# The last stages of a graph and LSTM kernel: one comparison per half for the gates, H doubled on ScalarE and added on GpSimd, four output buffers

## The chip, the cores and the metric

The kernel runs on one core of one Trainium2 chip. The metric is the device time of one execution in microseconds; given are the median of three runs and, beside it, one profiled execution from which the trace comes.

## What is computed

The program takes 6250 nodes with 256 features, adds a graph aggregation with two dense layers and a linear attention, and puts an LSTM with a small head on top. The change concerns only the head behind the LSTM:

```python
lstm_out = _lstm(x, W_ih, W_hh, b_ih, b_hh)
logits = jnp.einsum('bth,lh->btl', lstm_out, W_lin) + b_lin        # two logits per node
g = argmax(logits, axis=-1)[..., None]                             # 0 or 1
w = g * lstm_out
inc = jnp.cumsum(w, axis=1)
prefix = inc - w
suffix = inc[:, -1:, :] - inc
return 2.0 * lstm_out + prefix * fw_att + suffix * bw_att
...
x = x + _L0_ffn_ref(_layernorm(x)[None], ...)[0]
```

In the code H is `lstm_out`, kept in `hs`; the `x` of the last line is kept, transposed, in `x1T`; the running sum `inc` is in `cum`.

## The kernel before

All of this is feature by node: 128 partitions hold half of the 256 features, and the second half (c = 1) lies behind the first in the free dimension. The 6250 nodes are cut in NB = 25 blocks of BN = 250. The LSTM is solved in CH = 125 chunks of LS = 50 steps side by side, so `hs` is stored by step: partition, step, half, chunk. Node n = 50 j + t stands at step t + 1, chunk j. Two steps of all chunks are 250 columns and make a block of the gates; a block of the results is 250 neighbouring nodes, that is 5 chunks with all their steps, read from `hs` with a step of 250 elements.

After the LSTM's sweeps, which run in a loop that ends on a flag, three stages follow. Each engine runs its own instruction stream in order, and semaphores counted by block join them.

The gates. L1588 writes the four weight tiles `lin_rep` (two logits, two halves), each weight repeated over 128 columns, so that a matmul gives a logit already spread over all partitions. TensorE (`logits`, L805 to L812) makes both logits of a block in one of two PSUM banks, four matmuls in fp32, each of which the trace shows as two passes. ScalarE (L1077) copies the first logit with its bias to `lg0`. VectorE compares (L1593) and multiplies each half of H by the result (L1596), writing into `cum` in the order of the nodes, with a step of 50 elements. VectorE waits for its own comparison ahead of the products and for its own products at the end of each block.

The running sums. L1605 is one scan over 6250 columns for each half, with a column of ones as the multiplier, and L1609 multiplies the totals by `bwc`.

The results. For each block ScalarE computes the suffix part, L1092, from `cum` with scale `nbw` and bias `tbw`, into one of two buffers. VectorE adds 2 H to x (L1616, one for each half), adds the prefix part (L1622, one for each half) and the suffix part (L1626, both halves). TensorE (`rows`, L821 to L829) transposes the sum back to nodes by features in four transposes into one of two PSUM banks, ScalarE copies the bank to one of two output buffers (L1100), and SyncE stores it (L391). `results` waits for TensorE two blocks back, `rows` for ScalarE two blocks back, `suffix` for VectorE two blocks back, and `rows_out` for the store two blocks back. On ScalarE the order is suffix(i+1), rows_out(i), suffix(i+2), and so on. GpSimd's last work is L473, long before.

Of the kernel before, what the change touches and what calls it, by code (L numbers as in the profile page):

```python
# [9 lines left out]
ALU = mybir.AluOpType  # L10
ACT = mybir.ActivationFunctionType
AX = mybir.AxisListType.X
ds = bass.ds

P = 128
# [42 lines left out]
def build(nc, a, out):  # L58
# [7 lines left out]
    with ExitStack() as ctx:  # L66
# [88 lines left out]
        lin_rep = wih[:, 0:4 * P].rearrange("p (a m) -> p a m", a=4)  # L155
# [46 lines left out]
        lg0, gsel = [scr[:, v * BN:(v + 1) * BN] for v in range(2)], scr[:, 512:512 + BN]  # L202
        suf, res = part[2:4], part[4:6]
        outs = [w[0:TP, :].rearrange("p (t d) -> p t d", d=D) for w in (wq, wk)]
# [15 lines left out]
        def bank(b, c=2, w=BN, parts=P):  # L220
# [17 lines left out]
            "pe_swept", "lin_v", "lg_mm", "lg_act", "lg_g", "lg_v", "cum_v", "suf_act", "t_v", "out_mm", "out_act", "out_st0", "out_st1")}  # L238
# [35 lines left out]
        def _(sp):  # L274
# [114 lines left out]
            def store(i, par):  # L389
                sp.wait_ge(S["out_act"], i + 1)  # L390
                sp.dma_start(out[ds(i * BN, BN), :].rearrange("(t p) d -> p t d", p=TP), outs[par]).then_inc(S[f"out_st{par}"], 16)  # L391
            with sp.Fori(0, (NB - 1) // 2) as r:
                for u in range(2):
                    store(2 * r + u, u)
            store(NB - 1, 0)
            sp.wait_ge(S["out_st0"], 16 * ((NB + 1) // 2))
            sp.wait_ge(S["out_st1"], 16 * (NB // 2))
# [3 lines left out]
        def _(pool):  # L401
# [70 lines left out]
            for c in range(2):  # L472
                pool.tensor_copy(whb[c], whhv[:, c, :]).then_inc(S["w_low"], 1)  # L473

        @block.tensor
        def _(pe):
# [172 lines left out]
            pe.wait_ge(S["eps1_v"], 2)  # L650
# [153 lines left out]
            pe.wait_ge(S["lin_v"], 1)  # L804
            def logits(i, par, first):  # L805
                if not first:
                    pe.wait_ge(S["lg_g"], i - 1)
                for l in range(2):
                    for k in range(2):
                        last = mm(psum[:, 6 + par, l * BN:(l + 1) * BN], lin_rep[:, 2 * l + k, :],  # L810
                                  hs[:, ds(2 * i + 1, 2), k, :], start=(k == 0), stop=(k == 1))
                last.then_inc(S["lg_mm"], 1)  # L812
# [8 lines left out]
            def rows(i, par, first):  # L821
                pe.wait_ge(S["t_v"], 4 * i + 4)
# [16 lines left out]
        def _(act):  # L839
# [233 lines left out]
            def logits(i, par, first):  # L1073
                act.wait_ge(S["lg_mm"], i + 1)
                if not first:
                    act.wait_ge(S["lg_g"], i - 1)
                fn(lg0[par], psum[:, 6 + par, 0:BN], ACT.Identity, bias=blc[:, 0:1]).then_inc(S["lg_act"], 1)  # L1077
            logits(0, 0, True)
            logits(1, 1, True)
            with act.Fori(1, (NB - 1) // 2) as r:  # L1080
                for u in range(2):
                    logits(2 * r + u, u, False)
            logits(NB - 1, 0, False)

            act.wait_ge(S["cum_v"], 5)

            def suffix(i, par):

                if not isinstance(i, int) or i >= 2:
                    act.wait_ge(S["t_v"], 4 * i - 4)  # L1090
# [5 lines left out]
            def rows_out(i, par):  # L1096
                act.wait_ge(S["out_mm"], i + 1)
                if not isinstance(i, int) or i >= 2:
                    act.wait_ge(S[f"out_st{par}"], 8 * (i - par))
                fn(outs[par], psum[0:TP, par, :].rearrange("p (t d) -> p t d", t=2), ACT.Copy).then_inc(S["out_act"], 1)  # L1100

            suffix(0, 0)
            for i in (1, 2):
                suffix(i, i % 2)
                rows_out(i - 1, (i - 1) % 2)
            with act.Fori(0, (NB - 3) // 2) as r:
                for u in range(2):
                    suffix(2 * r + u + 3, 1 - u)
                    rows_out(2 * r + u + 2, u)  # L1110
            rows_out(NB - 1, (NB - 1) % 2)

        @block.vector
        def _(dve):
# [487 lines left out]
            gate(NB - 1, 0, False)  # L1603
            for c in range(2):
                dve.tensor_tensor_scan(cum[:, c, 1:N + 1], ones[:, 0:1].broadcast_to([P, N]), cum[:, c, 1:N + 1], 0.0,  # L1605
                                       ALU.mult, ALU.add).then_inc(S["cum_v"], 1)
            dve.wait_ge(S["cum_v"], 3)
# [4 lines left out]
            def results(i, par, first):  # L1612
                if not first:
                    dve.wait_ge(S["out_mm"], i - 1)
                for c in range(2):
                    last = stt(res[par][:, c, :].rearrange("p (j t) -> p j t", t=LS),  # L1616
                               hs[:, 1:LS + 1, c, ds(i * (BN // LS), BN // LS)].rearrange("p t j -> p j t"), 2.0,
                               x1T[:, c, ds(i * BN, BN)].rearrange("p (j t) -> p j t", t=LS), ALU.mult, ALU.add)
                last.then_inc(S["t_v"], 1)
                dve.wait_ge(S["t_v"], 4 * i + 1)  # L1620
                for c in range(2):
                    stt(res[par][:, c, :], cum[:, c, ds(i * BN, BN)], fwc[:, c:c + 1], res[par][:, c, :],  # L1622
                        ALU.mult, ALU.add).then_inc(S["t_v"], 1)
                dve.wait_ge(S["t_v"], 4 * i + 3)
# [32 lines left out]
```

## Time and profile before

| | us |
|---|---|
| median of 3 runs (lowest, highest) | 2604.55 (2603.65, 2613.02) |
| profiled execution | 2609.78 |
| its span, first to last instruction | 2607.9 |
| VectorE busy, whole span | 1761.6 |
| TensorE busy, whole span | 2304.9 |
| ScalarE busy, whole span | 1521.7 |
| GpSimd busy, whole span | 118.7 |
| gates, 2449.2 to 2505.2 | 56.0 |
| running sums, 2505.2 to 2531.5 | 26.3 |
| results, 2531.5 to the end | 76.4 |

PE is TensorE, PEld its weight loads, DVE VectorE, ACT ScalarE, POOL GpSimd, SP SyncE; a trailing q means the engine's sequencer. Times in the rows below are microseconds from the span's start, durations of one instruction in nanoseconds where a mean is given. In a timeline a row is start, duration, engine, line, operation, output and input, count, and in brackets how long the engine had been idle and what released it. A matmul's end is modelled.

### The profile page before, as it was taken

The page shows a single profiled execution, that of the slowest core. Times are in us where ns is not written, and L with a number is a line of the kernel's source. Part 1 is how long each engine was busy: PE and PEld are TensorE (multiplying, and loading weights), DVE is VectorE, ACT ScalarE, POOL GpSimd, SP SyncE. Part 2 cuts the span into 40 slices and gives each one's busy share as a digit, 9 for nine tenths or more (in the row PEclk, how much of TensorE's full clock was granted, in tenths as well). Part 3 has the DMA queues.
Part 4 walks back from the last instruction along what each step waited for, and adds up shares of the span by engine and source line. Part 5 has one row for each costly group of instructions (what it writes and reads, how often), then busy time and mean ns, then how long its engine had stood idle before and what let it go on. Part 6 is the DMA issues. An engine that isn't in the chain of part 4 may idle for free.

```text
span 2607.9 us, 46559 instructions
## 1 busy us (share of the span) xinstructions
PE 2304.9 (88%) x14839; PEld 1974.3 (76%) x14839; DVE 1761.6 (68%) x4053; ACT 1521.7 (58%) x2861; POOL 118.7 (5%) x121
## 2 busy tenths in 40 slices
PE   4578989999999999999898999998887887888844
PEld 3467868888888888888786888888887887888623
DVE  5755887777777777777477455556665665566688
ACT  2354448888888888888533444445554555555315
POOL 4232000000000000000000000000000000000000
PEclk9889999999999999999999999999999999999975
DMA  3222320000000000000331122123332332333103
GB/s 96 70 70 79 97 74 25 27 26 24 27 25 28 23 28 26 29 23 21 108 95 44 63 86 86 79 89 116 110 115 82 110 117 87 106 114 110 39 8 90
DMA packets 95188, 174.13 MB, mean 67 GB/s; under 512 B 8983, under 2 KB 69411, under 8 KB 94769
## 3 DMA queue, kind: packets, MB, share of 16 engines
q1 hardware_dynamic: 63378, 86.63, 10.1%
q10 hardware_dynamic: 28108, 81.19, 9.9%
q0 software_dynamic: 3584, 4.76, 0.6%
q8 instruction: 72, 1.18, 0.2%
q14 instruction: 46, 0.38, 0.0%
HBM read 114.14 MB, written 58.36 MB: 66 GB/s over the span
## 4 chain that ended last, share of the span: by engine, by line
PE 62%; DVE 14%; issue 8%; ACT 5%; ACTq 2%; DVEq 1%; POOL 0%; DMA 0%; POOLq 0%
PE psum L608 22%; PE psum L603 11%; PE psum L758 9%; PE psum L718 8%; DVE scr L1535 3%; DVE scr L1533 2%; ACT scr L1018 2%; PE psum L726 2%; PE psum L660 2%; PE psum L670 2%; PE psum L714 2%; DVE scr L1357 2%; DVE scr L1531 1%; DVE bufB L1537 1%; ACTq L1029 1%
## 5 line engine op out<-in xcount | busy, mean ns | idle before, releaser
L931 ACT ACTIVATE counts<-psum 125x500 fp32r<-125x500 f32 (+1 forms) x663 | 720.1, 1121 | 160.9 <-PE psum L603 159.1
L608 PE MATMUL psum<-halves,counts 125*125 125x512 f32 x2500 | 743.9, 418 | 2.8 <-ACT counts L931 2.0
L1383 DVE TENSOR_TENSOR wx<-rs_buf 128x500 bf16<-128x500 bf16 (+2 forms) x1326 | 641.9, 531 | 132.0 <-PE psum L603 72.2
L758 PE MATMUL psum<-bufB,wx 128*128 x4800 | 603.9, 283 | 90.6 <-DVE bufB L1537 81.6
L758 PEld LDWEIGHTS psum<-bufB,wx 128*128 128x128 f32 x4800 | 565.3, 194 | 129.0 <-issue 118.1
L608 PEld LDWEIGHTS psum<-halves,counts 125*125 125x125 f32 x2500 | 418.6, 187 | 59.9 <-issue 4.8
L603 PE MATMUL psum<-wx 128*125 128x250 bf16 x2550 | 399.3, 277 | 5.5 <-DVE wx L1383 5.3
L603 PEld LDWEIGHTS psum<-wx 128*125 128x125 bf16 x2550 | 320.9, 139 | 91.0 <-DVE wx L1383 8.6
L718 PE MATMUL psum<-bufA,wx 128*128 (+1 forms) x1600 | 232.7, 289 | 0.0
L718 PEld LDWEIGHTS psum<-bufA,wx 128*128 128x128 f32 x1600 | 194.9, 192 | 23.6 <-issue 0.2
L1018 ACT ACTIVATE scr<-scr 128x125 f32<-128x125 f32 x300 | 92.2, 307 | 168.6 <-DVE scr L1535 168.6
L1537 DVE TENSOR_TENSOR bufB<-scr 128x125 f32 (+1 forms) x300 | 87.1, 290 | 146.6 <-ACT scr L1018 146.6
L1531 DVE TENSOR_TENSOR scr<-scr 128x125 f32<-128x125 f32 x300 | 85.8, 286 | 84.6 <-ACT scr L1011 84.4
L1006 ACT ACTIVATE psum<-bufA 128x500 f32<-128x500 f32 x144 | 85.7, 595 | 95.6 <-ACT scr L1018 95.5
L1011 ACT ACTIVATE scr<-psum 128x250 f32<-128x250 f32 x300 | 110.0, 367 | 31.6 <-PE psum L758 31.6
L1525 DVE COPY psum<-bufA 128x500 f32<-128x500 f32 x144 | 97.7, 678 | 30.2 <-issue 30.1
L1490 DVE COPY bufB<-psum 128x250 f32<-128x250 f32 x192 | 75.2, 415 | 61.1 <-PE psum L718 59.0
L1535 DVE TENSOR_TENSOR scr<-scr 128x125 f32<-128x125 f32 x300 | 87.1, 290 | 10.3
L827 PE MATMUL psum<-ident,scr 128*125 128x128 f32 x100 | 30.4, 459 | 70.4 <-DVE scr L1626 70.4
L987 ACT ACTIVATE scr<-psum 128x250 f32<-128x250 f32 x50 | 19.0, 379 | 125.2 <-PE psum L726 125.2
L1533 DVE TENSOR_TENSOR scr<-scr 128x125 f32<-128x125 f32 x300 | 86.1, 287 | 5.6 <-ACT scr L1013 1.4
L1013 ACT ACTIVATE scr<-psum 128x125 f32<-128x125 f32 x300 | 81.5, 272 | 6.7 <-PE psum L758 1.4
(257 smaller groups left out, 2464.8 us busy)
## 6 DMA issues: line engine op xcount, KB each, us to landing
bufA<-gates_of_x ACTq DMA_DIRECT2D x144, 500.0 KB, 3.4
gates_of_x<-bufB SPq DMA_DIRECT2D x48, 500.0 KB, 2.6
sums_by_feature<-scr SPq DMA_DIRECT2D x51, 125.0 KB, 2.0
x_times_eps_plus_sums<-rs_buf ACTq DMA_DIRECT2D x10, 625.0 KB
wx<-in_x_dram SPq DMA_DIRECT2D x25, 250.0 KB
x_plus_mix<-wx SPq DMA_DIRECT2D x25, 250.0 KB, 4.8
scr<-x_times_eps_plus_sums SPq DMA_DIRECT2D x50, 125.0 KB
x_times_eps_plus_sums<-scr SPq DMA_DIRECT2D x50, 125.0 KB
```

The lines of the kernel that those rows point to most:

```text
L603: last = mm(psum[0:TP, u % 3, g * KEYS:(g + 1) * KEYS], oh_l[r][:, g, :, t], oh_m[r][:, g, :, t], start=(t == 0), stop=(t == 1))
L608: return mm(psum[0:TP, 3 + v, :], cnt[v][:, hi, :], xhl[:, hi, :, :].rearrange("p s d -> p (s d)"), start=(hi == 0), stop=(hi == NT - 1))
L718: last = mm(gate_bank(u, m), wihv[:, c, m * P:(m + 1) * P], ls_in[:, ds(t, 1), c, :].rearrange("p t j -> p (t j)"), start=False, stop=Fals ...
L758: return mm(half_gates(u, m, slot[0])[:, slot[1], :], whhv[:, k, (2 * gate + m) * P:(2 * gate + m + 1) * P], h, start=False, stop=(k == 1) ...
L931: fn(cnt[v][:, :, 2 * GW * u:2 * GW * u + GW * g].rearrange("p h c -> p c h"), psum[0:TP, u % 3, 0:g * KEYS].rearrange("p (c h) -> p c h", ...
L1011: fn(half(s_if, m), half_gates(u, m, 1), ACT.Sigmoid).then_inc(S["hif_act"], 1)
L1018: fn(th[:, m * CH:(m + 1) * CH], tg_c[1 - u][:, 1, m * CH:(m + 1) * CH], ACT.Tanh).then_inc(S["hth_act"], 1)
L1383: last = tt(to[:, 0:gs, :, :], tab2[:, 0:k, :].unsqueeze(1).broadcast_to([P, gs, k, 2]), keysT[v][:, part_, g0:g0 + gs, :].unsqueeze(2).br ...
L1531: tt(prod[:, 1, cut], s_if[:, 1, cut], tg_c[u][:, 1, cut], ALU.mult)
L1533: tt(prod[:, 0, cut], s_if[:, 0, cut], tg_c[u][:, 0, cut], ALU.mult).then_inc(S["prod_v"], 1)
L1535: tt(tg_c[1 - u][:, 1, cut], prod[:, 0, cut], prod[:, 1, cut], ALU.add).then_inc(S["hc_v"], 1)
L1537: tt(hs[:, ds(t + 1, 1), m, :].rearrange("p t j -> p (t j)"), s_o[:, cut], th[:, cut], ALU.mult).then_inc(S["hh_v"], 1)
```

## The change

The two logits are not compared any more; their difference is. The weights become half the difference of the two rows of W_lin, `lin_rep` has two tiles in place of four, and the bias is compared with it, so that TensorE has two matmuls a block, and one VectorE operation for each half compares and multiplies. ScalarE no longer copies a logit. Instead it doubles `hs` in place, 25 operations of two steps each, ahead of the matmuls that read them, and `fwc` and `bwc` are halved early in the program since the sums are then doubled. GpSimd adds the doubled H to `x1T` in place, 50 operations of 250 columns, after the last doubling, and VectorE's L1616 goes. The ones of the scan are read from PSUM. ScalarE's and SyncE's loops are written out; output buffers are four in place of two, two of them in `wv` and `wp`.

```diff
-        lin_rep = wih[:, 0:4 * P].rearrange("p (a m) -> p a m", a=4)
+        lin_rep = wih[:, 0:2 * P].rearrange("p (a m) -> p a m", a=2)
+        lin_d, b_d = sb("lin_d", 2), sb("b_d", 1)
...
-        outs = [w[0:TP, :].rearrange("p (t d) -> p t d", d=D) for w in (wq, wk)]
+        outs = [w[0:TP, :].rearrange("p (t d) -> p t d", d=D) for w in (wq, wk, wv, wp)]
...
@@ gpsimd
+            pool.wait_ge(S["twice_act"], NB)
+            for i in range(NB):
+                cells = x1T[:, :, i * BN:(i + 1) * BN].rearrange("p c (j t) -> p c j t", t=LS)
+                for c in range(2):
+                    pool.tensor_tensor(cells[:, c, :, :], cells[:, c, :, :],
+                                       hs[:, 1:LS + 1, c, i * (BN // LS):(i + 1) * (BN // LS)].rearrange("p t j -> p j t"),
+                                       ALU.add).then_inc(S["xh_q"], 1)
@@ tensor
-            pe.wait_ge(S["lin_v"], 1)
+            pe.wait_ge(S["lin_v"], 3)
             def logits(i, par, first):
+                pe.wait_ge(S["twice_act"], i + 1)
                 if not first:
-                    pe.wait_ge(S["lg_g"], i - 1)
-                for l in range(2):
-                    for k in range(2):
-                        last = mm(psum[:, 6 + par, l * BN:(l + 1) * BN], lin_rep[:, 2 * l + k, :],
-                                  hs[:, ds(2 * i + 1, 2), k, :], start=(k == 0), stop=(k == 1))
+                    pe.wait_ge(S["lg_v"], i - 1)
+                for k in range(2):
+                    last = mm(psum[:, 6 + par, 0:BN], lin_rep[:, k, :], hs[:, ds(2 * i + 1, 2), k, :],
+                              start=(k == 0), stop=(k == 1))
                 last.then_inc(S["lg_mm"], 1)
@@ scalar
-                fn(lg0[par], psum[:, 6 + par, 0:BN], ACT.Identity, bias=blc[:, 0:1]).then_inc(S["lg_act"], 1)
...
-            act.wait_ge(S["cum_v"], 5)
+            for i in range(NB):
+                fn(hs[:, 2 * i + 1:2 * i + 3, :, :], hs[:, 2 * i + 1:2 * i + 3, :, :], ACT.Copy, scale=2.0).then_inc(S["twice_act"], 1)
+
+            act.wait_ge(S["cum_v"], 6)
...
+                if i >= 4:
+                    act.wait_ge(S[f"out_st{i % 4}"], 16 * (i // 4))
+                fn(outs[i % 4], psum[0:TP, i % 2, :].rearrange("p (t d) -> p t d", t=2), ACT.Copy).then_inc(S["out_act"], 1)
@@ vector
+                ts(cols[:, 8:12], cols[:, 8:12], 0.5, None, ALU.mult).then_inc(S["eps1_v"], 1)
+                dve.wait_ge(S["eps1_v"], 2)
                 ts(nbw[:, :], bwc, -1.0, None, ALU.mult).then_inc(S["eps1_v"], 1)
...
-            dve.tensor_copy(lin_rep, lin_c[:, :].unsqueeze(2).broadcast_to([P, 4, P])).then_inc(S["lin_v"], 1)
+            tt(lin_d[:, :], lin_c[:, 2:4], lin_c[:, 0:2], ALU.subtract).then_inc(S["lin_v"], 1)
+            tt(b_d[:, :], blc[:, 0:1], blc[:, 1:2], ALU.subtract).then_inc(S["lin_v"], 1)
+            dve.wait_ge(S["lin_v"], 2)
+            ts(lin_rep, lin_d[:, :].unsqueeze(2).broadcast_to([P, 2, P]), 0.5, None, ALU.mult).then_inc(S["lin_v"], 1)
             dve.memset(cum[:, :, 0:1], 0.0).then_inc(S["cum_v"], 1)
+            dve.memset(psum[:, 4, 0:1], 1.0).then_inc(S["cum_v"], 1)
 
             def gate(i, par, first):
-                dve.wait_ge(S["lg_act"], i + 1)
-                stt(gsel[:, :], psum[:, 6 + par, BN:2 * BN], blc[:, 1:2], lg0[par], ALU.add, ALU.is_gt).then_inc(S["lg_g"], 1)
-                dve.wait_ge(S["lg_g"], i + 1)
+
+                dve.wait_ge(S["lg_mm"], i + 1)
                 for c in range(2):
-                    last = tt(cum[:, c, 1:N + 1].rearrange("p (j t) -> p t j", t=LS)[:, ds(2 * i, 2), :],
-                              hs[:, ds(2 * i + 1, 2), c, :], gsel[:, :].rearrange("p (t j) -> p t j", t=2), ALU.mult)
+                    last = stt(cum[:, c, 1:N + 1].rearrange("p (j t) -> p t j", t=LS)[:, ds(2 * i, 2), :],
+                               psum[:, 6 + par, 0:BN].rearrange("p (t j) -> p t j", t=2), b_d[:, 0:1],
+                               hs[:, ds(2 * i + 1, 2), c, :], ALU.is_gt, ALU.mult)
                 last.then_inc(S["lg_v"], 1)
-                dve.wait_ge(S["lg_v"], i + 1)
...
-                dve.tensor_tensor_scan(cum[:, c, 1:N + 1], ones[:, 0:1].broadcast_to([P, N]), cum[:, c, 1:N + 1], 0.0,
+                dve.tensor_tensor_scan(cum[:, c, 1:N + 1], psum[:, 4, 0:1].broadcast_to([P, N]), cum[:, c, 1:N + 1], 0.0,
...
             def results(i, par, first):
                 if not first:
                     dve.wait_ge(S["out_mm"], i - 1)
+                dve.wait_ge(S["xh_q"], 2 * i + 2)
                 for c in range(2):
-                    last = stt(res[par][:, c, :].rearrange("p (j t) -> p j t", t=LS),
-                               hs[:, 1:LS + 1, c, ds(i * (BN // LS), BN // LS)].rearrange("p t j -> p j t"), 2.0,
-                               x1T[:, c, ds(i * BN, BN)].rearrange("p (j t) -> p j t", t=LS), ALU.mult, ALU.add)
-                last.then_inc(S["t_v"], 1)
-                dve.wait_ge(S["t_v"], 4 * i + 1)
-                for c in range(2):
-                    stt(res[par][:, c, :], cum[:, c, ds(i * BN, BN)], fwc[:, c:c + 1], res[par][:, c, :],
+                    stt(res[par][:, c, :], cum[:, c, ds(i * BN, BN)], fwc[:, c:c + 1], x1T[:, c, ds(i * BN, BN)],
                         ALU.mult, ALU.add).then_inc(S["t_v"], 1)
```

## Rows read from the trace of the kernel before

**Rows 1.** Windows: us, busy of each engine (instructions), granted clock, DMA share, GB/s

```profile
2449.20:2505.20 56.00, 50.20 (x200) 37.58 (x200) 39.33 (x75) 11.72 (x25) 0.00 (x0) 0.96 0.00 0
2505.20:2531.50 26.30, 0.00 (x0) 0.00 (x0) 26.25 (x3) 0.00 (x0) 0.00 (x0) 0.50 0.00 0
2531.50:2607.90 76.40, 30.38 (x100) 23.00 (x100) 64.25 (x127) 39.19 (x75) 0.00 (x0) 0.50 0.28 84
```

**Rows 2.** Waits, 2452 to 2608: engine line waited for, total us, times, longest

```profile
PE psum L827 <- DVE scr L1626: 70.4, 25, 32.4
```

**Rows 3.** Timeline of the gates, two blocks in the steady state

```profile
2480.65 0.48 DVE L1593 SCALAR_TENSOR_TENSOR scr<-psum,cols,scr 128x250 f32<-128x250 f32 x1
...
2481.38 1.10 DVE L1596 TENSOR_TENSOR bufA<-bufB,scr 128x250 f32 x2 [0.25 <-DVE scr L1593]
...
2482.89 0.48 DVE L1593 SCALAR_TENSOR_TENSOR scr<-psum,cols,scr 128x250 f32<-128x250 f32 x1 [0.41 <-DVE bufA L1596]
...
2483.53 3.91 PE L810 MATMUL psum<-bufB,wx 128*128 x16 [0.28 <-DVE scr L1593]
...
2484.84 0.48 DVE L1593 SCALAR_TENSOR_TENSOR scr<-psum,cols,scr 128x250 f32<-128x250 f32 x1
```

**Rows 4.** Timeline of the results, one block in the steady state

```profile
2539.79 1.08 DVE L1616 SCALAR_TENSOR_TENSOR scr<-bufB,bufC 128x250 f32 x2
...
2541.00 0.87 DVE L1622 SCALAR_TENSOR_TENSOR scr<-bufA,cols,scr 128x250 f32<-128x250 f32 x2
2541.34 0.60 ACT L1100 ACTIVATE wq<-psum 125x512 f32<-125x512 f32 x1 [1.40 <-PE psum L827]
2541.84 1.07 ACT L1092 ACTIVATE scr<-bufA,tbw,nbw 128x250 f32 x2
2541.99 0.68 DVE L1626 TENSOR_TENSOR scr<-scr 128x500 f32<-128x500 f32 x1
...
2542.62 1.08 DVE L1616 SCALAR_TENSOR_TENSOR scr<-bufB,bufC 128x250 f32 x2
...
2542.72 1.22 PE L827 MATMUL psum<-ident,scr 128*125 128x128 f32 x4 [1.51 <-DVE scr L1626]
```

**Rows 5.** Groups by line and shape, whole span: count, busy us, mean ns

```profile
L970 ACT ACTIVATE wq<-scr 128x500 f32<-128x500 f32 x13 | 8.1, 620 | 45.9 <-DVE scr L1448 45.9
...
L1605 DVE TENSOR_TENSOR_SCAN bufA<-ones,bufA 128x6250 f32<-128x6250 f32 x2 | 26.2, 13166 | 0.0
...
L1243 DVE TENSOR_TENSOR bufC<-bufB,tab 101x4000 bf16<-101x4000 f32 x2 | 9.0, 4521 | 0.0
...
L440 POOL TENSOR_TENSOR scr<-scr 125x256 f32<-125x256 f32 x50 | 37.4, 748 | 62.7 <-DVE scr L1296 60.8
```

**Rows 6.** Windows of the gates' first and later part, columns as in rows 1

```profile
2449.20:2453.00 3.80, 3.79 (x9) 3.16 (x10) 0.00 (x0) 0.05 (x1) 0.00 (x0) 0.50 0.00 0
...
2456.00:2480.00 24.00, 22.57 (x95) 16.72 (x94) 17.91 (x36) 5.62 (x12) 0.00 (x0) 1.00 0.00 0
```

**Rows 7.** Timeline of the gates' start, TensorE and ScalarE

```profile
2449.21 13.15 PE L810 MATMUL psum<-bufB,wx 128*128 128x250 f32 x48 [0.52 <-DVE wx L1588]
2452.95 0.47 ACT L1077 ACTIVATE scr<-psum,cols 128x250 f32<-128x250 f32 x1 [9.66 <-PE psum L810]
```

**Rows 8.** Timeline of an early stage where GpSimd and VectorE work together

```profile
96.78 0.73 POOL L440 TENSOR_TENSOR scr<-scr 125x256 f32<-125x256 f32 x1 [1.53 <-DVE scr L1296]
96.95 1.23 DVE L1241 TENSOR_TENSOR bufB<-bufB,tab 101x640 bf16<-101x640 f32 x1
```

**Rows 9.** Timeline of the results' first and last steps

```profile
2531.52 0.34 DVE L1609 TENSOR_SCALAR tbw<-bufA,cols 128x1 f32<-128x1 f32 x2
...
2533.78 0.68 DVE L1626 TENSOR_TENSOR scr<-scr 128x500 f32<-128x500 f32 x1
...
2600.93 0.68 DVE L1626 TENSOR_TENSOR scr<-scr 128x500 f32<-128x500 f32 x1
...
2603.54 0.27 SPq L391 DMA_DIRECT2D out_dram<-wq  x1
```

More of the change, by code:

```diff
@@ L200, in build @@
         dif = rs_buf[:, 1616 + G4:1616 + G4 + 4 * (CH - 1)].rearrange("p (a j) -> p a j", a=4)
-        lg0, gsel = [scr[:, v * BN:(v + 1) * BN] for v in range(2)], scr[:, 512:512 + BN]
         suf, res = part[2:4], part[4:6]
-        outs = [w[0:TP, :].rearrange("p (t d) -> p t d", d=D) for w in (wq, wk)]
+        outs = [w[0:TP, :].rearrange("p (t d) -> p t d", d=D) for w in (wq, wk, wv, wp)]
         psum = ctx.enter_context(nc.psum_tensor("psum", [P, 8, 512], F32))
@@ L237, in build @@
             "hif_mm", "hgo_mm", "hif_act", "htg_act", "hc_v", "hth_act", "hh_v", "fill_a", "fill_d",
-            "pe_swept", "lin_v", "lg_mm", "lg_act", "lg_g", "lg_v", "cum_v", "suf_act", "t_v", "out_mm", "out_act", "out_st0", "out_st1")}
+            "pe_swept", "lin_v", "lg_mm", "lg_v", "xh_q", "twice_act", "cum_v", "suf_act", "t_v", "out_mm", "out_act", "out_st0", "out_st1", "out_st2", "out_st3")}
         ld_x = [sem(f"ld_x{v}") for v in range(XR)]
@@ L387, in _ @@
                                  pre_out[v].rearrange("p g n -> p (g n)")).then_inc(S[f"pre_st{v}"], 16)
-            def store(i, par):
+            for i in range(NB):
                 sp.wait_ge(S["out_act"], i + 1)
[L391 to L397, printed above, removed]
+                sp.dma_start(out[i * BN:(i + 1) * BN, :].rearrange("(t p) d -> p t d", p=TP), outs[i % 4]).then_inc(S[f"out_st{i % 4}"], 16)
+            for v in range(4):
+                sp.wait_ge(S[f"out_st{v}"], 16 * ((NB + 3 - v) // 4))
         @block.gpsimd
@@ L649, in _ @@
             pe.wait_ge(S["ld_w12"], 32)
-            pe.wait_ge(S["eps1_v"], 2)
+            pe.wait_ge(S["eps1_v"], 3)
             def tail(i, par, inner=False):
@@ L821, in rows @@
             def rows(i, par, first):
-                pe.wait_ge(S["t_v"], 4 * i + 4)
+                pe.wait_ge(S["t_v"], 3 * i + 3)
                 if not first:
@@ L1071, in _ @@
                 act.reg_mov(go, act.value_load(flag[0:1, 0:1], min_val=0, max_val=CH))
[L1073 to L1076, printed above, removed]
-                fn(lg0[par], psum[:, 6 + par, 0:BN], ACT.Identity, bias=blc[:, 0:1]).then_inc(S["lg_act"], 1)
[L1078 to L1083, printed above, removed]
-            act.wait_ge(S["cum_v"], 5)
+            for i in range(NB):
+                fn(hs[:, 2 * i + 1:2 * i + 3, :, :], hs[:, 2 * i + 1:2 * i + 3, :, :], ACT.Copy, scale=2.0).then_inc(S["twice_act"], 1)
+            act.wait_ge(S["cum_v"], 6)
             def suffix(i, par):
                 if not isinstance(i, int) or i >= 2:
-                    act.wait_ge(S["t_v"], 4 * i - 4)
+                    act.wait_ge(S["t_v"], 3 * i - 3)
                 for c in range(2):
@@ L1094, in suffix, with rows_out @@
                 last.then_inc(S["suf_act"], 1)
-            def rows_out(i, par):
+            def rows_out(i):
                 act.wait_ge(S["out_mm"], i + 1)
[L1098 to L1111, printed above, removed]
+                if i >= 4:
+                    act.wait_ge(S[f"out_st{i % 4}"], 16 * (i // 4))
+                fn(outs[i % 4], psum[0:TP, i % 2, :].rearrange("p (t d) -> p t d", t=2), ACT.Copy).then_inc(S["out_act"], 1)
+            for i in range(NB + 1):
+                if i < NB:
+                    suffix(i, i % 2)
+                if i:
+                    rows_out(i - 1)
         @block.vector
@@ L1603, in _ @@
             gate(NB - 1, 0, False)
+            dve.wait_ge(S["lg_v"], NB)
             for c in range(2):
-                dve.tensor_tensor_scan(cum[:, c, 1:N + 1], ones[:, 0:1].broadcast_to([P, N]), cum[:, c, 1:N + 1], 0.0,
+                dve.tensor_tensor_scan(cum[:, c, 1:N + 1], psum[:, 4, 0:1].broadcast_to([P, N]), cum[:, c, 1:N + 1], 0.0,
                                        ALU.mult, ALU.add).then_inc(S["cum_v"], 1)
-            dve.wait_ge(S["cum_v"], 3)
+            dve.wait_ge(S["cum_v"], 4)
             for c in range(2):
@@ L1614, in results @@
                     dve.wait_ge(S["out_mm"], i - 1)
+                dve.wait_ge(S["xh_q"], 2 * i + 2)
                 for c in range(2):
[L1616 to L1622 removed]
+                    stt(res[par][:, c, :], cum[:, c, ds(i * BN, BN)], fwc[:, c:c + 1], x1T[:, c, ds(i * BN, BN)],
                         ALU.mult, ALU.add).then_inc(S["t_v"], 1)
[L1624 removed]
+                dve.wait_ge(S["t_v"], 3 * i + 2)
                 dve.wait_ge(S["suf_act"], i + 1)
```

## The prediction, made before the changed kernel was run

> **What bounds the kernel now.** Only the last 160 us of the program are touched, so I read those and nothing else. The busy times by stage come first [rows 1]: three stages stand there, the gates (56.0 us), the running sums (26.3 us) and the results (76.4 us). In the first, TensorE is busy 50.20 of 56.00 us, which looks like a TensorE bound; in the second only VectorE works; in the third VectorE is busy 64.25 of 76.40 us and everybody else waits, TensorE 70.4 us for L1626 [rows 2]. GpSimd does nothing in any of them.
>
> The timeline of the gates in their steady state [rows 3] corrects the first reading. Two blocks take 2484.84 - 2480.65 = 4.19 us, 2.10 a block. TensorE's 16 records for two blocks take 3.91 us, so 1.95 a block, and VectorE's own sequence is 0.48 (L1593), 0.25 idle, 1.10 (two L1596) and a turn of 0.12 (0.41 at the loop's end), so 1.95 to 2.24. VectorE is the one without slack, and TensorE would be there a moment later. Both have to shrink, and the change shrinks both.
>
> In the results [rows 4] a block takes VectorE 2542.62 - 2539.79 = 2.83 us: L1616 until L1622 starts 1.21, L1622 twice and a wait 0.99, L1626 until the next block 0.63. ScalarE has 0.50 (L1100) and 1.07 (L1092), TensorE 1.22 at half clock (0.50 in the stage's row [rows 1]).
>
> **Part 1, the preparation.** One copy (L1588) becomes two tiny subtractions, a wait and a scaling, with a one-element memset more. No such row stands in the last stages; from the gap of 0.25 between dependent VectorE operations [rows 3] I take 0.4 us more (bounds 0.1 and 0.8). The early halving of two vectors lies beside loads of the first microseconds: nothing, and at most 0.4 if that cover is gone.
>
> **Part 2, doubling on ScalarE.** 25 operations of 128x500 from SBUF to SBUF. The nearest row is L970, 620 ns [rows 5]. Since an operation starts 0.10 before the former's end (L1100 lasts 0.60, its follower starts after 0.50 [rows 4]), the pitch is 0.52, in all 13.0 us from about 2448.9 to 2461.9. ScalarE's 11.7 us of L1077 go in exchange. TensorE waits for the first doubling only, and that is over when the weights are written; later blocks are ready at 0.52 each while the stage needs over 1.0 each. No cost; if ScalarE started 1 us late, 1 us.
>
> **Part 3, the gates.** TensorE has two matmuls in place of four, so 0.98 a block at full clock. VectorE loses L1593 and has two operations with a PSUM input and the strided output of L1596. The trace has no such form. Lower bound for the pair: two plain ones, 0.87 (L1622 [rows 4]); upper: L1596 plus what the strided read adds in L1616, 1.10 + (1.08 - 0.87) = 1.31. I take L1596's 1.10, the same output pattern at the same length, because L1593 shows that a PSUM input costs nothing (0.48 against half of 0.87 plus an overlap). There are two PSUM banks, so block i+2 waits for the gate of block i; the loop is 0.98 (TensorE) + 0.25 (wait and register work ahead of VectorE) + 1.10 + 0.28 (VectorE to TensorE [rows 3]) = 2.61 for two blocks, 1.31 a block. VectorE alone would need 1.1, TensorE 0.98. With a little of the loop's turn I take 1.32 (bounds 1.05 and 1.60). The first two blocks run at 1.2 GHz: the first stretch has clock 0.50 and the later ones 1.00 [rows 6], and the first block's eight passes took from 2449.21 to 2452.95 [rows 7], so four take 1.87. Stage: 0.4 + 2 x 1.87 + 0.25 + 1.10 + 23 x 1.32 + 0.25 before the sums = 36.1 us, against 56.0: 19.9 saved.
>
> TensorE's clock: its busy share falls from 0.90 to about 0.98/1.32 = 0.74. At 1.2 GHz it would itself be the bound, busy without a gap, and it was from just such a stretch that it rose to 1.00 [rows 6].
>
> **Part 4, the sums.** The constant operand moves from SBUF to PSUM. L1605 takes 13166 ns for 6250 elements [rows 5], 2.11 ns each, where a tensor_tensor with two SBUF inputs runs at 4521/4000 = 1.13 (L1243), so it isn't the second input that slows it. Nothing gained or lost (bounds -1 and +1 us).
>
> **Part 5, GpSimd's 50 additions.** They start when all doublings are done, at 2461.9. L440, a tensor_tensor of 125x256, takes 0.72 us undisturbed (its mean of 748 ns has a few longer ones in it) [rows 5, 8]. The new one reads one input with a stride; on VectorE that turned a pair of 0.87 into 1.08 [rows 4], a factor of 1.25, so 0.90 (bounds 0.70 and 1.40, the second twice the plain one). 50 x 0.90 = 45 us: done at 2507. The results begin at 2449.2 + 36.1 + 26.3 + 0.3 = 2511.9. So the additions lie wholly beside gates and sums up to (2511.9 - 2461.9)/50 = 1.00 us apiece. Beyond that they don't merely deliver late (at 1.8 us a block and two operations a block they keep ahead up to 1.7), they collide with VectorE.
>
> That collision is in this trace: L1241, 640 columns with two SBUF inputs, took 1.23 us where L1243's rate gives 0.72; it had started 0.17 us into a GpSimd addition and ended 0.67 after it [rows 8]. It waited for GpSimd to end. The Trainium skill (SBUF — State Buffer, section "Who interferes with whom") says the same: a VectorE instruction with two SBUF inputs contends with a GpSimd one that reads SBUF, the pair of ports is a lock held for a whole instruction, and one with at most one SBUF input does not contend. The rule speaks against this change where GpSimd is still at it in the results, whose three operations all have two SBUF inputs, and for it in gates and sums, where one input now is in PSUM. No row here shows the second half. By the rule the sum stays what it is; against it the sums would hold GpSimd off, which is a rival below.
>
> **Part 6, the results.** VectorE loses L1616: 2.83 - 1.21 = 1.62 us a block. ScalarE needs 1.57. But with both so near, a loop through all three engines ends last. The scratch buffers alternate: the L1626 of block i releases TensorE (0.05), TensorE transposes (1.22), ScalarE moves the block out (0.04 + 0.50), only then computes the suffix of block i+2 (1.07), and only then comes L1626 of block i+2 (0.03 + 0.68) [rows 4]. That is 3.59 for two blocks, and the loop turn on TensorE brings 0.04 more: 3.63, 1.82 a block. So of the 1.21 taken from VectorE 1.0 arrives. From the first L1626's end (2534.46) to the last's (2601.61) are 67.15 us [rows 9]; it becomes 12 x 3.63 = 43.6, 23.5 saved. Before the first one, ScalarE's suffix (0.04 + 0.33 + 1.07) and L1626 (0.68) after the sums' scale need 2.15 where 2.94 passed (2531.52 to 2534.46 [rows 9]): 0.8 saved. The last steps, 6.3 us from there to the span's end, stay.
>
> Four output buffers: the last store is issued about 2.0 us after the last L1626's end, and the span ends 6.3 after it [rows 9], so a store has landed within 4.4 us. With two buffers it would have 2 x 1.82 - 0.5 = 3.1 us, with four 6.8. Two would have become a new wait; four hide it. Store traffic goes from 84 to about 130 GB/s, DMA share from 0.28 to 0.45 [rows 1].
>
> **Sum.** 19.9 + 0.8 + 23.5 = 44.2 us. Against the profiled execution's 2609.78 us (span 2607.9, so 1.9 outside it) that makes 2565.6; the median of the runs shown is 2604.55, 5.2 lower, and 44.2 off that makes **2560.3 us**.
>
> **The rivals.**
> GpSimd's additions run into the results. Each tenth over 1.00 us brings 5 us of overlap, in which VectorE and GpSimd take turns. At 1.2 us apiece: 10 us more, 2570; at 1.4: 2580. For it: no strided GpSimd operation stands in the trace. Against: a third more than the plain one is already allowed for.
> The sums hold GpSimd off. After 36.1 - 12.7 = 23.4 us of gates 26 additions are done, 24 x 0.90 = 21.6 us remain behind the sums: up to 2582. For it: 13 us instructions would hold any lock long; against: one input has left SBUF.
> TensorE's clock stays at 1.2 GHz in the gates: 1.95 a block, 23 x 0.63 = 14.5 us more, 2575. Against: it is then fully busy.
> The clock rises in the results, where TensorE's share goes from 0.40 to 0.67: the loop is 0.6 shorter for two blocks and ScalarE and VectorE bound at 1.65; 4 us less, 2556. It lies within the forecast's range.
> VectorE's pair is near 0.87 and the waits overlap: 1.05 a block, 6 us less; with the former 2550.
> Slower than before: one mechanism, GpSimd's price. The overlap eats all 44.2 us from 50 x (g - 1.00) = 44, g = 1.88 us, 2.6 times the plain addition. At 2.4 us the time is 2630. For it: an access with a 1000-byte step could be handled element by element; against: VectorE's price for that very step is 0.11 us an operation.
>
> **How the numbers follow.** Forecast (2551 to 2569) 0.66; additions into the results, 2569 to 2585, 0.14; sums hold GpSimd 0.05; low clock in the gates 0.05; faster than 2551 0.05; slower than before 0.03; something between 2591 and 2617 0.02. The range 2549 to 2577 leaves out about 0.17. Faster or slower by over 0.5% (13 us, about what a measurement of this kernel can tell from no change): 0.94, 0.03, 0.03.
>
> **What the changed profile would show.** Gates: blocks 1.32 us apart, new pair 1.10, clock 1.00 after two blocks. Sums: still 26.3. GpSimd: 50 operations of 0.90, ended before the sums do. Results: blocks 1.82 apart, VectorE with about 0.2 us idle a block waiting for ScalarE's suffix, TensorE at 0.50. I'm wrong if GpSimd works past the first L1626, if VectorE's operations in the results grow beyond 0.48 and 0.68, if the doublings set the pace of the gates, or if ScalarE waits for a store.

## The result and the profile after

| | before | after |
|---|---|---|
| median (lowest, highest) | 2605.3 (2603.65, 2613.02), 4 runs | 2584.42 (2582.09, 2585.76), 4 runs |
| ratio, 95% interval | | 0.9913 (0.9892, 0.9934) |
| profiled execution, span | 2609.78, 2607.9 | 2585.76, 2583.9 |

The kernel is faster by 20.9 us. 44.2 us were forecast (2560.3, range 2549 to 2577): the sign was right, the size was not, and the time lies outside the range. Set against the forecast for the profiled execution (2565.6) there are 20.2 us too many.

What stands ahead of the changed stages scatters from one execution to the next by some us. So a second measure stands beside the times in this text, read from the trace: the stretch from TensorE's first instruction behind the sweeps to the end of the span, called the last stages. It is 159.4 us before and 133.2 us after, 26.2 us less.

These are the windows of the three stages after the change, columns as in rows 1, and under them a stretch well inside the results:

```profile
2451.50:2488.60 37.10, 28.07 (x100) 18.41 (x100) 28.01 (x51) 11.84 (x24) 25.19 (x32) 0.94 0.00 0
2488.60:2514.90 26.30, 0.00 (x0) 0.00 (x0) 26.26 (x3) 0.00 (x0) 15.39 (x20) 0.53 0.00 0
2514.90:2583.90 69.00, 30.36 (x100) 22.98 (x100) 37.35 (x77) 39.06 (x75) 0.00 (x0) 0.50 0.29 93
2530.00:2560.00 30.00, 15.17 (x52) 11.60 (x51) 18.19 (x38) 19.32 (x39) 0.00 (x0) 0.50 0.33 108
```

Gates and sums are about where they were forecast (37.1 us for 36.1, 26.3 for 26.3). The results take 69.0 us in place of the 52 that the sum has for them, and there every engine is idle for a good part of the time (VectorE busy 37.35 of 69.00). The number to look at is easily missed: the DMA share, 0.33. The experiments below show that it is a ceiling. GpSimd's 50 additions form this group (count | busy us, mean ns | idle before):

```profile
L475 POOL TENSOR_TENSOR bufC<-bufC,bufB 128x250 f32<-128x250 f32 x50 | 40.6, 854 | 1029.5 <-ACT bufB L1078 1029.5
```

The gates after, in the timeline, answer to rows 3. A cycle of two blocks is 2472.38 - 2469.57 = 2.81 us; TensorE's eight passes are 1.99 of it, VectorE's four operations 2.15, and both wait for each other once a cycle. The first two rows, from earlier in the stage, show what one block costs when it stands alone, first start to last end: 1.11 us for TensorE's four passes, 1.17 us for VectorE's two operations.

```profile
2458.37 1.11 PE L814 MATMUL psum<-bufB,wx 128*128 x4 [0.31 <-DVE bufA L1591]
...
2459.73 1.17 DVE L1591 SCALAR_TENSOR_TENSOR bufA<-psum,b_d,bufB 128x250 f32 x2 [0.24 <-PE psum L814]
...
2469.57 2.15 DVE L1591 SCALAR_TENSOR_TENSOR bufA<-psum,b_d,bufB 128x250 f32 x4 [0.56 <-PE psum L814]
...
2471.02 1.99 PE L814 MATMUL psum<-bufB,wx 128*128 x8 [0.73 <-DVE bufA L1591]
...
2472.38 2.15 DVE L1591 SCALAR_TENSOR_TENSOR bufA<-psum,b_d,bufB 128x250 f32 x4 [0.65 <-PE psum L814]
```

The results begin as forecast. These rows answer to rows 4; they show VectorE waiting 0.50 us for ScalarE's suffix, and ScalarE's copy-out starting as soon as TensorE's transposes end:

```profile
2518.66 1.22 PE L831 MATMUL psum<-ident,scr 128*125 128x128 f32 x4 [0.28 <-DVE scr L1617]
...
2519.92 0.60 ACT L1095 ACTIVATE wk<-psum 125x512 f32<-125x512 f32 x1
2520.02 0.68 DVE L1617 TENSOR_TENSOR scr<-scr 128x500 f32<-128x500 f32 x1 [0.50 <-ACT scr L1087]
```

L1617 is the last operation of a block on VectorE (L1626 before). For the first nine blocks its ends are alternately 1.58 and 2.08 us apart, 3.66 for two blocks against 3.63 forecast. Then ScalarE's copy-out begins to wait for a store out of the buffer that it is to fill, for each of the four buffers in turn, and two blocks take 4.6 to 5.2 us. The first of these waits:

```profile
2532.15 0.60 ACT L1095 ACTIVATE wp<-psum 125x512 f32<-125x512 f32 x1 [1.18 <-DMA out_dram<-wp]
```

After the last store's issue at 2574.47 the span goes on for 9.4 us, 4.4 in the kernel before [rows 9]. SyncE's own waits (2574 to 2584; total, times, longest) show three stores landing one after another, the third 2.1 us behind these two:

```profile
SPq L393 <- DMA out_dram<-wv: 3.2, 1, 3.2
SPq L393 <- DMA out_dram<-wp: 2.8, 1, 2.8
```

So the stores have queued up. In the steady part a block takes about 2.49 us.

### The profile page after: what moved, and what is told of

Same layout as the page of the kernel before. It is cut to its first block, busy times and chain, and to the rows that moved or that the text cites. A ratio compares the mean times of both kernels' runs of the same rounds, so it can differ in the third digit from the quotient of the medians.

```text
span 2583.9 us, 46053 instructions
## 1 busy us (share of the span) xinstructions
PE 2285.2 (88%) x14739; PEld 1956.3 (76%) x14739; DVE 1720.4 (67%) x3982; ACT 1523.0 (59%) x2861; POOL 159.2 (6%) x171
## 4 chain that ended last, share of the span: by engine, by line
PE 59%; DVE 15%; issue 7%; ACT 6%; DMA 2%; ACTq 2%; DVEq 1%; POOL 0%; SPq 0%; POOLq 0%
PE psum L612 23%; PE psum L607 11%; PE psum L762 9%; PE psum L722 8%; DVE scr L1527 3%; DVE scr L1525 2%; ACT scr L1022 2%; PE psum L730 2%; DMA out_dram<-wq 2%; DVE scr L1349 2%; PE psum L718 2%; DVE wp L1445 2%; DVE scr L1523 1%; DVE bufB L1529 1%; ACTq L1033 1%
## 5 line engine op out<-in xcount | busy, mean ns | idle before, releaser
L722 PEld LDWEIGHTS psum<-bufA,wx 128*128 128x128 f32 x1600 | 194.9, 192 | 23.6 <-issue 0.2
L475 POOL TENSOR_TENSOR bufC<-bufC,bufB 128x250 f32<-128x250 f32 x50 | 40.6, 854 | 1029.5 <-ACT bufB L1078 1029.5
```

What stands on the lines that cost most here:

```text
L722: last = mm(gate_bank(u, m), wihv[:, c, m * P:(m + 1) * P], ls_in[:, ds(t, 1), c, :].rearrange("p t j -> p (t j)"), start=False, stop=Fals ...
```

## The experiments

```profile
DMA packets 6376, 6.41 MB, mean 76 GB/s; under 512 B 125, under 2 KB 6375, under 8 KB 6375
```

The other count goes by the packets' starts and durations: from 2540 to 2565 us five packets are under way for 64% of the time and six for 25%, never none and never over nine (successive records overlap a little). Five at once is 0.31 of 16 engines; the mean of the records, 5.3, is the share of 0.33.

**Each store in two transfers, 120 and 5 partitions.**

```diff
-                sp.dma_start(out[...].rearrange("(t p) d -> p t d", p=TP), outs[i % 4]).then_inc(S[f"out_st{i % 4}"], 16)
+                to = out[...].rearrange("(t p) d -> p t d", p=TP)
+                for lo, hi in ((0, 120), (120, TP)):
+                    sp.dma_start(to[lo:hi, :, :], outs[i % 4][lo:hi, :, :]).then_inc(S[f"out_st{i % 4}"], 16)
```

> The changed kernel, each store of a block in two transfers: partitions 0 to 119 and 120 to 124 (the buffer is free when both have landed). Theory A: one transfer whose outer dimension is 125 is spread over 5 of the 16 DMA engines only (125 divides by 5 and by no greater number up to 16; the changed kernel's DMA share stands at 0.33 to 0.34 while stores queue, about 5/16), so a store takes about 2.45 us and that is the pace of the results. 120 divides by 15, so the stores should no longer bound: blocks 1.83 us apart to the end, no wait of ScalarE for a store, 10 us less in the blocks and about 6 in the tail, 2569 us. Rival B, the rate of writes to HBM (100 to 117 GB/s seen): no gain, 2584. Rival C, the latency of each store with four in flight: no gain, 2584, or a little slower for the second transfer.

2566.23 us (2559.77 to 2567.55), ratio 0.9839 (0.9820, 0.9858): 18 us less than the changed kernel. The last stages take 115.3 us, 17.9 less. No wait for a store is left, blocks go at 1.58 and 2.08 to the end, and the span ends 3.0 us after the last store's issue. There are 20 small packets for each store, 15 and 5. The same 30 us as above:

```profile
2530.00:2560.00 30.00, 19.90 (x66) 15.19 (x67) 24.06 (x49) 24.51 (x48) 0.00 (x0) 0.50 0.54 141
```

141 GB/s are written where 108 were: rival B is out.

**The same split in the kernel before.**

> The kernel before, with the same split of its stores. Theory A: its blocks are 2.82 us apart, longer than the 2.45 us that a store on 5 engines takes, so the pace stays at 2.82; only the last store lands sooner: 1 to 3 us less, 2603. Rivals B and C: no change, 2605. If the blocks come closer than 2.82 us, the stores bound the kernel before already, which none of these says. Its early part also tells whether the 2.2 us that the changed kernel lost ahead of its last stages are noise between executions.

2607.73 us, ratio 0.9993 (0.9981, 1.0004). Its blocks stay 2.80 and 2.83 us apart: the kernel before was not bound by its stores. It was close, though. This is the steady part in the trace of the kernel before, with stores unsplit:

```profile
2550.00:2580.00 30.00, 12.73 (x43) 9.79 (x44) 27.32 (x54) 16.79 (x33) 0.00 (x0) 0.50 0.30 92
```

That is 0.30 at 92 GB/s, and the changed kernel's queue is at its limit with 0.33 and 104 to 112 GB/s. Five packets were under way for 58% of this stretch already, and none for 2%. The gain of 1 to 3 us that I had expected behind the last block can't be told in the median, but it stands in the trace: the span ends 3.0 us after the last store's issue in place of 4.4, and the last stages take 157.9 us, 1.5 less.

**Eight output buffers, stores unsplit** (four more in `wx`, which is free by then).

```diff
-        outs = [... for w in (wq, wk, wv, wp)]
+        outs = [... for w in (wq, wk, wv, wp)] + [wx[0:TP, 2048 + 512 * v:2560 + 512 * v]... for v in range(4)]
```

> The changed kernel with eight output buffers in place of four, stores unsplit. Theory A and rival B (a pace of about 2.45 us a store, whatever the buffers): the engines run ahead for some 25 blocks and the stores drain behind them; the end stays within 2 us of the changed kernel, 2583. Rival C (latency with four in flight): with eight in flight no wait is left, 2569.

2585.29 us (2573.28 to 2587.3), the changed kernel's time; the last stages take 133.4 us for 133.2. VectorE's last operation ends 44.2 us after its first block's, nearly as it does with no wait at all (44.0 in the split kernel), and then the stores drain with almost nobody else at work:

```profile
2560.00:2578.00 18.00, 0.14 (x1) 0.00 (x0) 0.00 (x0) 0.61 (x2) 0.00 (x0) 0.50 0.31 98
```

With eight stores in flight the end comes no earlier. It is a rate, not a latency: rival C is out.

**Control: the cut at partition 115.**

```diff
-                for lo, hi in ((0, 120), (120, TP)):
+                for lo, hi in ((0, 115), (115, TP)):
```

> e1_split's control: also two transfers a store, but cut at partition 115 (115 divides by 5 and by nothing greater up to 16, 10 goes to 10 engines). If what helped in e1_split was having two transfers in flight: 2566. If it is the number of engines: a store costs 115/125 of 2.49 and its small part, 2.3 to 2.4 us, the results go at that pace, and the time is 2577 to 2583.

2575.3 us (2571.15 to 2581.87), 9 us over the cut at 120. But it is also 9 us below the changed kernel, and the last stages take 121.9 us, where the cut at 120 takes 115.3 and the unsplit store 133.2. So this control alone can't separate two transfers from more engines. The blocks go at 2.05 us where waits are, faster than the 2.3 I had worked out. From 2540 to 2560 more than five packets are under way for 69% of the time, which a small second transfer of 10 partitions doesn't explain. What does, is open; the next two experiments do without a second transfer.

**One transfer a store, 120 partitions; one transfer a store, 115 partitions** (rows left out of the output).

```diff
-                sp.dma_start(out[...].rearrange("(t p) d -> p t d", p=TP), outs[i % 4]).then_inc(S[f"out_st{i % 4}"], 16)
+                to = out[...].rearrange("(t p) d -> p t d", p=TP)
+                sp.dma_start(to[0:120, :, :], outs[i % 4][0:120, :, :]).then_inc(S[f"out_st{i % 4}"], 16)   # or 0:115
```

> The changed kernel, each store one transfer of partitions 0 to 119 only: the rows of five partitions in every 125 are left out of the output. One transfer as in the changed kernel, 4% less to write, but an outer dimension that 15 divides. Theory A (number of engines): no waits for stores, 2565, DMA share over 0.5. If it takes two transfers to go faster: about 2581, 4% off the stores' pace.

> The same with partitions 0 to 114 (the rows of ten partitions in every 125 left out): 8% less to write, but 5 is the greatest divisor up to 16. Theory A: still 5 engines, stores at 0.92 x 2.5 = 2.3 us, DMA share 0.31 to 0.33, 2578 to 2581, slower than e9_one120 though it writes less. If engines don't matter: no slower than e9_one120.

2564.77 us (2560.61 to 2567.97) for 120 and 2573.73 (2570.3 to 2576.09) for 115: the kernel that writes less takes 9 us more. The last stages take 115.1 and 126.7 us. The window 2530 to 2560 of 120 with its count of packets, then the window of 115:

```profile
2530.00:2560.00 30.00, 20.16 (x67) 15.44 (x68) 24.77 (x50) 25.27 (x51) 0.00 (x0) 0.50 0.51 132
```

```profile
DMA packets 6376, 6.15 MB, mean 58 GB/s; under 512 B 375, under 2 KB 6375, under 8 KB 6375
```

```profile
2530.00:2560.00 30.00, 16.46 (x55) 12.63 (x56) 20.17 (x42) 21.30 (x42) 0.00 (x0) 0.50 0.33 109
```

0.33 is the ceiling for 125 and for 115; 120 goes past it. A store of 120 has 375 / 25 = 15 small packets, one of 115 has 5 again. The pace at 115 is 2.3 us, 0.92 of 2.49. The time came out lower than the 2578 to 2581 that I had expected of it, but that was ahead of the last stages: these are 6.5 us shorter than the changed kernel's, and 6.5 off its 2584.4 is 2577.9. All of this is theory A, and it is what the Trainium skill states (DMA: Bandwidth & Descriptors, section "Why a DMA increments its semaphore by 16 and not by 1"): the number of engines that a transfer uses is the largest up to 16 that divides the outer dimension of both of its sides, which for 125 is 5 and for 120 is 15. The traces agree with it in both cases, by the small packets and by the shares of 0.33 and 0.51. They do not name the engines.

**Two output buffers, unsplit and split** (the split as in the first experiment).

```diff
-        outs = [... for w in (wq, wk, wv, wp)]
+        outs = [... for w in (wq, wk)]
...
-                if i >= 4:
-                    act.wait_ge(S[f"out_st{i % 4}"], 16 * (i // 4))
+                if i >= 2:
+                    act.wait_ge(S[f"out_st{i % 2}"], 16 * (i // 2))
```

> The changed kernel with two output buffers in place of four, stores unsplit. The prediction's step: two buffers would have 3.1 us where a store needs up to 4.4 to land, so they become a wait, four hide it. With stores on 5 engines I now expect that four hide little: the pace is the stores' either way, 2.5 us or a little more, 2584 to 2592.

> e1_split with two output buffers. In e1_split the last store is issued 3.0 us ahead of the span's end, so it lands in less; 2 x 1.83 - 0.6 = 3.0 us are there between the issue and the next use of its buffer. 2566 to 2570: with stores on 15 engines two buffers nearly do. If two are short after all: over 2575.

2582.38 us (2576.95 to 2586.14) unsplit and 2566.98 (2563.67 to 2569.08) split; the last stages take 132.5 and 115.3 us. These are the times of four buffers in both cases (133.2 and 115.3), so the four buffers of the change are worth nothing measurable. With stores on 5 engines they only move the first wait for a store, from the third block's copy-out to the eighth's; with stores on 15 two are enough.

**ScalarE's order, then four PSUM banks for the gates.** First, on top of the split, the suffix of block i+2 goes ahead of the copy-out of block i:

```diff
-            for i in range(NB + 1):
+            for i in range(NB + 2):
                 if i < NB:
                     suffix(i, i % 2)
-                if i:
-                    rows_out(i - 1)
+                if i >= 2:
+                    rows_out(i - 2)
```

> As e1_split, and ScalarE's order in the results changed: the suffix of block i+2 ahead of the copy-out of block i. My theory of the pace without the stores is the loop VectorE L1617, TensorE transposes, ScalarE copy-out, ScalarE suffix, 3.63 us for two blocks. The new order takes TensorE and the copy-out off it; VectorE's own 1.62 us a block is left. Blocks 1.65 us apart instead of 1.83, 4.5 us less than e1_split, 2565. If the loop is not what binds (VectorE or ScalarE alone): the time of e1_split.

2561.06 us (2557.41 to 2566.17). The ranges of this kernel and the split one overlap, but the traces are clear: the last stages take 110.5 us, 4.8 less, and the ends of VectorE's last operation are 1.58 and 1.71 us apart. That is 1.64 a block, where I expected 1.65 once TensorE and the copy-out are off the loop. Second, on top of that:

```diff
-                    pe.wait_ge(S["lg_v"], i - 1)
+                    pe.wait_ge(S["lg_v"], i - 3)
...
-                    last = mm(psum[:, 6 + par, 0:BN], lin_rep[:, k, :], ...
+                    last = mm(psum[:, GB4[v], 0:BN], lin_rep[:, k, :], ...      # GB4 = (6, 7, 2, 3)
```

> e4_split_order and four PSUM banks for the gates (banks 6, 7, 2, 3, a wait for the gate four blocks back in place of two). My theory: the gates' blocks are 1.40 us apart because the loop TensorE 0.98, to VectorE 0.38, the pair 1.08, back to TensorE 0.36 is 2.80 us for the two banks. With four banks VectorE's pair alone is left, 1.08 us a block: 23 x 0.32 = 7 us less in the gates, 2554 us in all. Rival: VectorE's waits and register work bind, not the banks: the time of e4_split_order, 2561. A second rival: TensorE, then waiting for nothing, is itself at 0.98 to 1.1, same answer as the theory.

2550.37 us (2544.51 to 2554.39), ratio 0.9769 (0.9755, 0.9782), five runs: the fastest of all. The last stages take 101.6 us, 8.9 less than with two banks. In the gates VectorE hardly waits any more:

```profile
2456.00:2479.00 23.00, 21.16 (x91) 15.79 (x90) 22.86 (x47) 7.56 (x15) 15.36 (x19) 0.99 0.00 0
```

VectorE is busy 22.86 of 23.00 us and TensorE 21.16; a block takes about 1.0 us, a little less than the 1.08 I had. Which of the two sets that pace, this run doesn't tell.

**The ones of the sums in SBUF again.**

```diff
-                dve.tensor_tensor_scan(cum[:, c, 1:N + 1], psum[:, 4, 0:1].broadcast_to([P, N]), ...
+                dve.tensor_tensor_scan(cum[:, c, 1:N + 1], ones[:, 0:1].broadcast_to([P, N]), ...
```

> e1_split with the ones of the running sums read from SBUF again, as in the kernel before, so that each scan has two SBUF inputs while GpSimd adds. If such an instruction holds GpSimd off for its whole length: some 31 additions are done when the sums begin, about 19 x 0.86 = 16 us of them follow behind the sums and collide with the results, and the time is 2575 to 2582. If not: 2566, as e1_split, and the PSUM operand was worth nothing. The scans keep 13.17 us each in both.

2582.98 us (2578.68 to 2586.03), 17 us over the split kernel; the last stages take 130.7 us, 15.4 more. The size was right, the direction wrong. The first scan is the one held up, GpSimd goes on as before. The two scans (shortest, median and longest, in ns), and the stretch in which the first one runs beside the additions:

```profile
L1603 DVE TENSOR_TENSOR_SCAN bufA<-ones,bufA x2: 13147/20836/28524, 2487.2 to 2515.6; 128x6250 f32<-128x6250 f32 x2
```

```profile
2487.15:2502.70 15.55, 0.00 (x0) 0.00 (x0) 15.55 (x1) 0.00 (x0) 15.49 (x20) 0.54 0.00 0
```

The first scan takes 28.5 us and the second 13.1, 15.4 more in all. That is as long as GpSimd's last 19 additions, which run on undisturbed (median 864 ns, one starting every 0.81 us). After the last of them the first scan lasts another 13.0 us, about a scan's full length, so it had done next to nothing until then. With these additions beside the sums, the PSUM operand is worth 15.4 us.

**GpSimd's additions behind the sums.**

```diff
-            pool.wait_ge(S["twice_act"], NB)
+            pool.wait_ge(S["cum_v"], 4)
```

> e1_split with GpSimd's additions waiting until both running sums are made, so that they lie wholly beside the results. It prices the collision that the prediction named. Without any contention GpSimd delivers a block in 1.72 us, less than the results' 1.83: 2 us more than e1_split, 2568. With whole-instruction locks against VectorE's three operations, all with two SBUF inputs: about 2 x 0.86 + 1.62 = 3.3 us a block in place of 1.83, 37 us more, 2603.

2590.9 us (2589.04 to 2593.14), 25 us over the split kernel, between my two cases; the last stages take 138.9 us, 23.6 more. While additions last, a block takes 3.22 us and both sides get slower. The additions (shortest, median and longest, in ns), and one block of the timeline:

```profile
L477 POOL TENSOR_TENSOR bufC<-bufC,bufB x50: 845/1028/1296, 2516.7 to 2568.5; 128x250 f32<-128x250 f32 x50
```

```profile
2533.45 1.12 DVE L1619 TENSOR_TENSOR scr<-scr 128x500 f32<-128x500 f32 x1
2534.49 2.05 DVE L1615 SCALAR_TENSOR_TENSOR scr<-bufA,cols,bufC 128x250 f32 x2
...
2536.67 1.12 DVE L1619 TENSOR_TENSOR scr<-scr 128x500 f32<-128x500 f32 x1
```

In 3.22 us there are three VectorE operations and three additions (50 of them in 52.8 us). The counts say that the two take turns, at 1.07 us a pair; alone, VectorE's operations last 0.47 and 0.68 us and an addition starts every 0.81. I had let GpSimd do two additions a block; it does three, is through after some 17 blocks, and the rest goes at the usual pace. A collision costs each of VectorE's operations about 0.5 us.

This is not what the scan met. There one operation of VectorE waited for 19 additions, here each waits for one, and in both GpSimd had a row of additions ready. What decides between the two, no run shows.

## Why the prediction was wrong, and where it was right

The step that failed is in part 6, the output buffers: "so a store has landed within 4.4 us. ... Two would have become a new wait; four hide it. ... DMA share from 0.28 to 0.45". It took the time from issue to landing for all that a store costs, and a share of 0.45 for something that these stores could reach. A ring of buffers hides a latency; it can't hide a rate. The stores came out of 5 engines, whose ceiling in this measure is 0.33 and about 2.49 us a store, and the forecast's pace of 1.82 us lay beyond it. The term that the sum had at nothing, the wait for stores, measured 16.9 us.

The signs stood in the trace of the kernel before: a share of 0.28 over the stage in rows 1, 0.30 in its steady part, five packets under way for most of the time. The outer dimension of 125 stood in its code. "ScalarE waits for a store" stood among what would show me wrong, without a price and a chance: a rival was missing, and the range with it. The measured 2584.4 lies in the band of another rival, the additions that run into the results (2569 to 2585). That is chance: they ended 11 us before the results began.

Where the 20.2 us come from, by the timelines:

| | forecast | after | too many |
|---|---|---|---|
| TensorE's first instruction behind the sweeps | 2448.5 | 2450.7 | 2.2 |
| from there to the sums | 36.8 | 37.9 | 1.1 |
| sums | 26.3 | 26.3 | 0.0 |
| to the first L1617's end | 2.15 | 2.24 | 0.1 |
| first to last L1617 | 43.6 | 54.0 | 10.4 |
| to the span's end | 6.3 | 12.8 | 6.5 |

The first line is within the scatter: in the experiments that instruction starts between 2447.5 and 2453.7, at 2453.7 with the kernel before's own code up to there. Whether the change adds anything ahead of the last stages isn't shown; it saves 26.2 us within them, and the medians are 20.9 apart.

The last two lines are the stores, 16.9 us, and the split kernel gives 17.9 back. Its last stages take 115.3 us, where the forecast's lines behind the first add up to 115.2. That agreement is in part luck: its gates take 1.1 us more than forecast, and its end 1.4 less, since its last store is through in 3.0 us and not in 4.4.

The other steps, in the order of the prediction:
- Preparation: 0.14 us more than before from TensorE's first instruction to the first matmul, 0.4 taken.
- Doubling: 25 operations in 12.86 us (L1078), 13.0 taken. It never held TensorE. The profile names it twice, for 0.28 and 0.39 us, but the doubling of those blocks had ended several us before; what had just ended was VectorE's pair two blocks back.
- Gates: 1.40 us a block in place of 1.32. The loop over two PSUM banks was the right mechanism, as four banks showed. Its two hand-overs are as taken, 0.25 us to VectorE and 0.27 back (0.25 and 0.28). What was too small are the two pieces of work: TensorE's four passes take 1.11 us from first start to last end, not 0.98, and VectorE's pair 1.17, not 1.10. 1.11 + 0.25 + 1.17 + 0.27 is the measured 2.8 us (a matmul's end is modelled, so where TensorE's 1.11 ends and the hand-over begins is rough). The 0.98 was a pace, what a block adds when passes follow one another; a loop that hands over waits for the last end. With four banks the pace counts again, 1.0 us a block. The granted clock was 0.50 up to 2456 and 1.00 from there to 2480.
- Sums: 13164 ns a scan, as before, and that beside 19 running additions. So the half that part 5 said no row shows is shown here: a VectorE instruction with one input in PSUM kept clear of GpSimd. That the operand gains nothing was true only of a scan by itself; beside the additions it is worth 15.4 us. The rival had the collision the other way round, with GpSimd held off.
- Additions: 854 ns, one starting every 0.81; 0.90 taken. They ended at 2504, 11 us ahead of the results. The slower-than-before rival needed 1.88 us, over twice that. (Part 5 says that at two a block they keep ahead of the results up to 1.7 us; from its own numbers, 50 us ahead and 24 blocks of 1.8, it is 1.9. Nothing hung on it.)
- Results without stores: 1.83 us a block, 1.82 taken. The loop through three engines was confirmed by ScalarE's new order, which gives 1.64.
- TensorE stayed at 0.50 (1.2 GHz) in the results, also in the split kernel, where it is busy 19.90 of 30.00 us. The rival of a rising clock there didn't come.

## What to carry to other kernels

When a stage is made faster, ask of each transfer in it how many DMA engines it uses, not only when it lands: divide the measured DMA share by the share of engines that its outer dimension allows. Here 125 partitions made 5 of 16, 0.31, and a share of 0.30 left almost no room. Cutting five partitions off into a second transfer gave 18 us, where the whole change had given 21. A second input in PSUM, even a constant, kept VectorE's scan clear of GpSimd; here that was worth the length of the 19 additions that GpSimd still had to do. And in a loop between two engines count each piece of work from its first start to its last end, not by its pace.

## What the runs showed of the hardware

- The stores reach 104 to 112 GB/s with an outer dimension of 125 and 109 with 115, and the DMA share stops at 0.33 in both. With 120 they reach 132 GB/s, and with 120 and 5 in two transfers 138 to 156, not at their limit. The small packets for each store are 5, 5, 15 and 20.
- A scan with two SBUF inputs that met a row of GpSimd additions waited for the last of them (15.4 us), not for the current one. Shorter VectorE operations with two SBUF inputs took turns with the additions, one each, at 1.07 us a pair. Each was seen in one kernel.
- A scan with one of its inputs in PSUM took 13164 ns beside such additions, as long as by itself.
- VectorE's operation of the gates, with a PSUM input and an output step of 200 bytes, took 660 ns (median) where L1596, with both inputs in SBUF and the same output step, took 633. The two are different operations, so how much of the 27 ns is the PSUM input isn't shown.
